# Weight loads and their waits moved into the norms' SyncE programs, and the last feed-forward layer storing its own output

## The reference, cut to what matters

```python
x = x + _L0_attn_a_ref(_layernorm(x, axis=-1), ...)
x = x + _L0_ffn_ref(_layernorm(x, axis=-1), ...)
x = x + _L0_attn_b_ref(_layernorm(x, axis=-1), ...)
x = x + _L0_ffn_ref(_layernorm(x, axis=-1), ...)
...
x = x + _L3_attn_b_ref(_layernorm(x, axis=-1), ...)
x = x + _L3_ffn_ref(_layernorm(x, axis=-1), ...)
return x
```

## Time and profile before

| | |
|---|---|
| Median of three runs | 3286.94 us |
| Lowest and highest | 3273.81 us, 3288.47 us |
| Profiled execution, its own time | 3289.86 us |
| Span of that execution, first to last instruction | 3288.1 us |
| Time outside the span | 1.76 us |
| Granted TensorE clock, mean over the span | 0.922 |
| TensorE busy, share of the span | 86% |
| VectorE, ScalarE, GpSimd busy | 56%, 42%, 23% |

### The profile page before, as it was taken

The page is one execution under the profiler, slowest core; times in us unless marked ns, Lnnn a source line. Parts: engine busy times, 40 slices in busy tenths (PEclk is TensorE's granted clock), DMA queues, the critical chain, the costliest instruction groups (busy, mean ns, idle before and its releaser), DMA issues. The chain is left out here.

```text
span 3288.1 us, 54460 instructions
## 1 busy us (share of the span) xinstructions
PE 2822.4 (86%) x21112; PEld 1419.8 (43%) x21112; DVE 1848.9 (56%) x3584; ACT 1366.0 (42%) x2665; POOL 765.5 (23%) x725
## 2 busy tenths in 40 slices
PE   6667788999988888899678888998889898889988
PEld 3454465333466433344322222342233444565546
DVE  4425553798763688311598888212594544537633
ACT  3314244422243376632367677422204232234552
POOL 1000063365354200000653230002550001230003
PEclk9779599899999899999789999998899998898989
DMA  3031011122012311000312100000430001031102
GB/s 119 16 100 47 13 42 48 60 70 67 11 49 87 76 30 27 2 0 0 66 26 34 24 12 1 1 0 15 112 103 0 1 1 52 21 101 36 33 2 78
DMA packets 84392, 130.03 MB, mean 40 GB/s; under 512 B 15584, under 2 KB 52928, under 8 KB 82856
## 3 DMA queue, kind: packets, MB, share of 16 engines
q1 hardware_dynamic: 71528, 106.68, 12.1%
q0 software_dynamic: 9152, 16.71, 2.1%
q10 hardware_dynamic: 3456, 3.15, 0.3%
HBM read 99.93 MB, written 25.85 MB: 38 GB/s over the span
## 5 line engine op out<-in xcount | busy, mean ns | idle before, releaser
L1811 DVE TENSOR_REDUCE at_mp<-PS 128x1 f32<-128x384 f32 (+3 forms) x640 | 307.0, 535 | 94.6 <-PE PS L1632 82.7
L1760 ACT ACTIVATE at_pt<-PS 128x384 f32<-128x384 f32 (+3 forms) x704 | 272.5, 455 | 198.0 <-PE PS L1632 163.7
L1624 PE MATMUL PS<-at_kx,at_qx 48*128 48x384 bf16 (+5 forms) x640 | 203.1, 354 | 37.2 <-DVE at_mp L1811 21.6
L113 PE MATMUL PS<-zeros 128*128 128x512 bf16 x834 | 208.6, 396 | 1.2 <-DVE mx_y L982 1.2
L1652 PE MATMUL PS<-at_qx,at_kx 57*128 57x512 bf16 (+5 forms) x704 | 196.5, 320 | 9.8 <-ACT at_pt L1760 9.4
L4335 ACT ACTIVATE ls_pt<-PS,ls_far 128x512 f32<-128x512 f32 x256 | 155.4, 684 | 22.5 <-PE PS L4156 18.1
L1632 PE MATMUL PS<-at_above,identb 64*128 64x128 bf16 (+1 forms) x1408 | 164.4, 216 | 0.0
L4482 DVE CUSTOM_DVE_ANT_0 PS<-PS,ls_pt 128x1024 f32<-128x1024 f32 x128 | 153.7, 1239 | 18.1 <-ACT ls_pt L4335 15.5
L1632 PE MATMUL PS<-at_other,at_eye 64*128 64x128 bf16 (+1 forms) x1408 | 162.2, 213 | 0.0
L2540 DVE TENSOR_TENSOR_SCAN mb_ring<-PS,mb_ring 128x1024 f32<-128x1024 f32 x64 | 146.6, 2290 | 18.9 <-POOL mb_ring L2473 6.7
L1133 DVE SCALAR_TENSOR_TENSOR X<-PS,small_L,X 128x512 f32<-128x512 f32 x8 | 6.0, 750 | 261.2 <-PE PS L1080 261.2
(11 more groups left out here) (839 smaller groups left out, 6330.6 us busy)
## 6 DMA issues: line engine op xcount, KB each, us to landing
rw_arena<-rw_v_rows SPq DMA_DIRECT2D x32, 512.0 KB, 4.7
dl_arena<-in_fir_bank SPq DMA_DIRECT2D x32, 256.0 KB, 3.2
lnA<-mb_rows SPq DMA_DIRECT2D x16, 512.0 KB, 3.7
XN<-mb_rows SPq DMA_DIRECT2D x16, 512.0 KB, 3.7
ffn_place<-in_ffn_L SPq DMA_DIRECT2D x4, 1152.0 KB, 17.0
x_rows<-mx_t SPq DMA_DIRECT2D x16, 256.0 KB, 2.5
mx_s<-y_rows SPq DMA_DIRECT2D x16, 256.0 KB, 5.0
ffn_place<-in_ffn_L SPq DMA_DIRECT2D x4, 1024.0 KB, 8.0
```

Of the source, the lines that this page charges most:

```text
L113: k.nc.tensor.matmul(k.PS[:, bank, :], k.zeros16[:, 0:P], k.zeros16[:, :], start=start, stop=start, skip_group_check=True)
L1624: mm = nc.tensor.matmul(PS[:, n % 3, 0:e - c], QX[rows, u % 3, g, blk(i, P)], KX[rows, u % 3, g, c:e], start=True, stop=True)
L1760: nc.scalar.activation(PT[:, y % SLOTS, g, 0:e - c], PS[:, 3 + n % 3, 0:e - c], ACT.Exp, scale=SCALE).then_inc(exp_done, 1)
L1811: nc.vector.tensor_reduce(best, sc, AX.X, ALU.max).then_inc(s_maxed, 1)
```

## The change

It does three things.

- `weights_beside` is a new SyncE program inside `layernorm` and `layernorm_twice`. If a group's weights are due to be loaded (`k.ffn_next`), it issues the four DMAs there, in the norm of the next sub-layer. Otherwise, if the sub-layer is a feed-forward layer (`k.ffn_due`), it waits there for the loads. Otherwise it does nothing.
- The three stages of `load_ffn` after feed-forward layers and the eight stages of `await_loads` ahead of feed-forward layers go. The load at the start and the two waits at the start stay.
- When the last sub-layer is `l3_ffn`, its SyncE program stores each block of `X` as soon as VectorE has added it, with two more semaphores in that stage (`x_done`, `stored`); the stage "stored" at the end goes. In `l3_ffn`, VectorE's wait behind each of the four adds becomes one wait behind all four.

```diff
+def weights_beside(k, sp):
+
+    if k.ffn_next is not None:
+        layer, k.ffn_next = k.ffn_next, None
+        n = pack_columns(FFN_W[layer])
+        for c in range(LOAD_PARTS):
+            part = slice(c * n // LOAD_PARTS, (c + 1) * n // LOAD_PARTS)
+            sp.dma_start(k.ffn_place[:, part], k.ins["ffn_" + layer][:, part]).then_inc(k.ffn_loaded, 16)
+        k.ffn_count += 16 * LOAD_PARTS
+    elif k.ffn_due:
+        sp.wait_ge(k.ffn_loaded, k.ffn_count)
...
+        @block.sync
+        def _(sp):
+            weights_beside(k, sp)
...
+                if k.last_output is not None:
+                    for b in range(NBLK):
+                        sp.wait_ge(x_done, b + 1)
+                        sp.dma_start(k.last_output[:, blk(b)], k.X[:, blk(b)]).then_inc(stored, 16)
+                    sp.wait_ge(stored, 16 * NBLK)
...
-                    own(nc.vector.tensor_tensor(k.X[:, blk(b)], k.X[:, blk(b)], PS[:, b, :], ALU.add))
+                    nc.vector.tensor_tensor(k.X[:, blk(b)], k.X[:, blk(b)], PS[:, b, :], ALU.add).then_inc(x_done, 1)
+                dve.wait_ge(x_done, NBLK)
...
-            if name.endswith("ffn"):
-                await_loads(k, k.ffn_loaded, k.ffn_count)
+            k.ffn_due = name.endswith("ffn")
+            k.last_output = out if i == last - 1 and name == "l3_ffn" else None
             with ExitStack() as layer:
                 run[name](k)
             if name.endswith("ffn") and i + 2 < last and SUBLAYERS[i + 2] != name:
-                load_ffn(k, SUBLAYERS[i + 2][0:2].upper())
-        with stage(nc, "stored") as (block, stored):
-            @block.sync
-            def _(sp):
-                for b in range(NBLK):
-                    sp.dma_start(out[:, blk(b)], k.X[:, blk(b)]).then_inc(stored, 16)
-                sp.wait_ge(stored, 16 * NBLK)
+                k.ffn_next = SUBLAYERS[i + 2][0:2].upper()
+                weight_views(k, k.ffn_place, FFN_W[k.ffn_next])
+        if k.last_output is None:
+            with stage(nc, "stored") as (block, stored):
...
```

More of the change, by code:

```diff
@@ L318, in l3_ffn @@
                    "rows_stored", "x_turned", "x_copied", "hid_ready", "hid_done", "y_ready", "y_taken",
-                   "diag_made", "block_0", "block_1", "block_2", "block_3", "mixed", "own_d") as (
+                   "diag_made", "block_0", "block_1", "block_2", "block_3", "mixed", "x_done", "stored", "own_d") as (
                        block, cleared, logits_ready, shifted, exp_done, picked, ranked, counted, in_tile, in_place, named, numbered, found, placed, turned, rows_copied,
                        rows_stored, x_turned, x_copied, hid_ready, hid_done, y_ready, y_taken,
-                       diag_made, block_0, block_1, block_2, block_3, mixed, own_d):
+                       diag_made, block_0, block_1, block_2, block_3, mixed, x_done, stored, own_d):
             back = (block_0, block_1, block_2, block_3)
@@ L4656, in program @@
     k = Core(nc)
-    k.ins, k.ffn_count = ins, 0
+    k.ins, k.ffn_count, k.ffn_next = ins, 0, None
     k.filled_count, k.fetched_count = 0, [0] * 8
@@ L4699, in program, with _ @@
             if name.endswith("ffn") and i + 2 < last and SUBLAYERS[i + 2] != name:
-                load_ffn(k, SUBLAYERS[i + 2][0:2].upper())
-        with stage(nc, "stored") as (block, stored):
-            @block.sync
-            def _(sp):
-                for b in range(NBLK):
-                    sp.dma_start(out[:, blk(b)], k.X[:, blk(b)]).then_inc(stored, 16)
-                sp.wait_ge(stored, 16 * NBLK)
+                k.ffn_next = SUBLAYERS[i + 2][0:2].upper()
+                weight_views(k, k.ffn_place, FFN_W[k.ffn_next])
+        if k.last_output is None:
+            with stage(nc, "stored") as (block, stored):
+                @block.sync
+                def _(sp):
+                    for b in range(NBLK):
+                        sp.dma_start(out[:, blk(b)], k.X[:, blk(b)]).then_inc(stored, 16)
+                    sp.wait_ge(stored, 16 * NBLK)
 def layout(inputs):
```

## The result

The changed kernel took 3262.44 us (median of 8 runs, 3253.16 to 3265.36) where the kernel before took 3287.66 us (8 runs, 3273.81 to 3293.07). The ratio is 0.9932, 95% interval 0.9912 to 0.9952: 22 us less. The forecast was 16.0 us less and 3271 us; 3262 us lies in the stated range of 3259 to 3281. Two repeats of the changed kernel gave 0.9934 (0.9912 to 0.9956) and 0.9922 (0.9900 to 0.9944).

What follows compares the result with a forecast made beforehand. TensorE is busy 86% of the span, but boundaries, where every engine idles, were what the change touches. Stages and stores 12.1 us plus clock 3.9 us gave 16.0 us less than 3286.94: 3271 us, range 3259 to 3281.

Steps and rivals of the forecast that it cites:

- The stages' length: At eleven boundaries, removing the eight awaiting stages saves 2.8 us and the three loading stages 7.0 us.
- the one that was priced apart: The awaiting stage into the second l2_ffn, said to cost 0.65 us where the other seven cost 0.31 each.
- The end: At the program's end, storing each block once added saves 2.3 us, between 1.7 and 2.5.
- The 0.2 us for stores beside the row loads: In the last l3_ffn, a row load behind a store could land late; 0.2 us taken off the end's 2.5.
- the forecast's signs of being wrong: A norm longer than its twin through SyncE, line 432 waiting over 0.54 us for `mx_yg`, or as many norms at 0.8 clock.
- The clock at the loads: Norms behind the loading boundaries regain clock: 2.5 us at l3a, 0.1 at l2a, 0 at l1a.
- The clock at the waits: Norms behind the eight awaiting boundaries regain clock with 0.31 us less idle time: 1.3 us, between −1 and 5.4.
- a quarter of the 5.4, 1.3 us: First l3_ffn's and first l2_ffn's norms, near an edge, could each win 2.7 us; a quarter of both was taken.
- rival C: The clock gives more, both edge norms and l1a's stay at 1.00: 21.6 us less, 3265 us; chance 0.18.
- Rival B: The clock gives nothing, falls are dealt out anew: 12.1 us less, 3275 us, up to 3281; chance with E 0.28.
- D: Not faster: clock falls land in stretches bound by TensorE, deciding from 12.1 us of such stretches; chance 0.04.
- E: The weight load runs into l1a's main stage and holds its DMAs: 1 to 3 us off the 12.1; chance with B 0.28.

Runs made afterwards that it cites:

- e1_loads: The kernel before with only the three weight loads moved into the norms, awaiting stages and storing stage kept: ratio 0.9967, 10.8 us less.
- e2_waits: The kernel before with only the eight waits moved into the norms, loading stages and storing stage kept: ratio 0.9971, 9.5 us less.
- e9_before_fill: The kernel before, all small stages kept, plus products of zeros on TensorE behind the last matmuls of eight kinds of sub-layer: ratio 0.9976, 7.9 us less.
- e4_warm_loads: The kernel before with nine products of zeros on TensorE inside each of the three loading stages, no stage removed: ratio 0.9985, 4.9 us less.
- c2_after: The changed kernel repeated unaltered under another name: 3259.8 us, ratio 0.9934 against the kernel before.
- e6_fill: The changed kernel plus products of zeros on TensorE behind sub-layers' last matmuls, beside VectorE's last adds: 3252.32 us, ratio 0.9912 against the kernel before.
- c1_before: The kernel before repeated unaltered under another name: 3281.41 us, ratio 0.9996.
- e3_end: The kernel before with only the last layer's own stores changed, all small stages of the loads kept: ratio 1.0001.
- e5_empty: The changed kernel with empty stages (a barrier and nothing in it) put back at the eleven boundaries: ratio 0.9962 against the kernel before.
- e10_empty_front: The changed kernel with eleven empty stages in a row ahead of the first sub-layer: ratio 0.9949 against the kernel before.

## Why the prediction was right, and which term was too small

**The stages' length** held. The boundaries of the changed kernel show 0.33 us less at an awaiting stage (0.85 to 0.52 into the first l3_ffn) and 0.66 at the one that was priced apart (1.19 to 0.53). 2.8 us for the waits and 7.0 for the loads were read off the boundaries, the boundaries came out as forecast (1.27 us into l3a, 2.90 into l1a), and e1_loads alone gave 10.8 us where the sum had 7.0 + 2.5 + 0.1 = 9.6 for that part. The moved DMAs were hidden in the norm as argued, at 357 GB/s, and nobody waited for SyncE.

**The end** was sized at 2.3 us and measured 5.36 − 2.8 = 2.5 us. The 0.2 us for stores beside the row loads can't be seen in the traces. One of the forecast's signs of being wrong did come up: line 459 waited 0.72 us for `mx_yg` in the changed kernel. It says nothing, because without the new stores the same matmuls waited 0.99 us in e2_waits and 0.62 in e9_before_fill.

**The clock at the loads** was sized at 2.6 us. The loads' stretches went from 44.3 to 34.5 us, 9.8 us, of which 7.0 are the stages: 2.8 us of clock. l3a's 2.5 us came in every trace of the changed kernel, l2a's norm stayed at GpSimd's 11.7, and l1a's gave little, as said. e4_warm_loads shows the cause at l3a, on one trace; e9_before_fill's norm there, with a shorter idle time and the stage in place, is at 10.3 us too.

**The clock at the waits** is the term that was mis-sized. The prediction took "a quarter of the 5.4, 1.3 us". The waits' stretches went from 106.6 to 99.1 us, 7.5 us, of which 2.8 are the stages: 4.7 us of clock, with the standard error of 1.8. The step looked for norms near an edge by the idle time ahead of them and found two. It passed over the first l1_ffn's and the second l3_ffn's, both with 0.79 us of idle time, behind an attention layer whose tail already ran at the low level. Over the same traces they went from 12.1 to 10.3 and from 12.7 to 10.8 us with their stages, so beyond the 0.31 us some 1.5 us each. And of the two it named, it took a quarter for both alike, where the first l3_ffn's norm went from 12.1 to 10.3 us and was at 1.00 in every trace without the stage, while the first l2_ffn's went from 11.9 to 11.5 only.

That the idle time at these very boundaries did it is shown less well than the sum. The 8 us ahead of the first l1_ffn's and the second l3_ffn's norm, in the kernel before and in the changed one (two and two windows, columns as in the earlier trace rows):

```profile
1378.40:1386.40 8.00, 5.46 (x12) 1.70 (x10) 1.38 (x2) 0.60 (x1) 0.00 (x0) 0.50 0.00 0
3184.20:3192.20 8.00, 5.44 (x11) 1.66 (x9) 1.50 (x2) 0.60 (x1) 0.00 (x0) 0.50 0.00 0
...
1370.50:1378.50 8.00, 4.10 (x16) 1.76 (x16) 1.75 (x4) 1.24 (x3) 0.00 (x0) 1.00 0.00 0
3163.40:3171.40 8.00, 5.72 (x12) 1.72 (x10) 1.50 (x2) 0.66 (x2) 0.06 (x1) 0.50 0.00 0
```

Into the second l3_ffn the tail is low in both, and the clock rises sooner in the norm of the changed kernel (0.93 over it, not 0.80). Into the first l1_ffn the clock fell over 7 us ahead of the norm, so the boundary behind can't have started the fall: it fell there in all seven traces with the stage and in only two of the seven without (c2_after, e6_fill). At most the boundary can delay the return; why the tail kept the clock in the other five is not shown. The first l3_ffn's norm was low in only three of the seven traces with its stage (before, c1_before, e3_end), and in those l3a's norm was low too. In e1_loads, e4_warm_loads, e5_empty and e9_before_fill it ran at 1.00 with the stage in place. Part of its gain may thus belong to the loads' side of the change.

With 7.5 + 9.8 + 2.5 the three parts add up to 19.8 us, where the ratio of 0.9932 is 22.4 us of 3287.66 (interval 15.8 to 28.9). The sum is between the forecast's 16.0 and rival C's 21.6 us, with other norms than C named; the interval of the time holds both. Rival B, the clock gives nothing, would leave 12.1 us, which lies outside that interval, and the stretches of both parts speak against it. D and E did not happen. The Trainium skill says in TensorE: Matmul & The Clock Gate (section What's actually happening) that the number of matmuls at the low clock differs between runs of one kernel. The traces agree, since c1_before's norms fell out otherwise than those of before, but the mean moved all the same.

**What stays open.** l3b's main stage, which the change does not touch, took 225.7 to 227.9 us in all six traces without a stage ahead of the feed-forward layers and 230.1 to 243.3 in the seven with one; e10_empty_front, made to tell why, gave 229.4. The difference is in how long the clock stays low in it: the granted clock over it was 0.87 in the kernel before, 0.92 in the changed one and 0.83 in e1_loads, the longest. The means are 235.6 and 227.1 us, 8.5 us in favour of the change, of which the sum above leaves room for 2.6, or for 9.1 at the upper end of the interval. The other main stages did not grow to make up for it: but for the last one, they sum to 0.7 us less in the six traces, with a standard error of 2.6. A clean split of thirteen traces into these seven and six would come by chance once in 1716 ways. The grouping was made after the traces were seen, so the odds are less extreme than that, but chance is the weaker reading. What in the change would do it was not found, and e1_loads and e2_waits may hold part of it in their times. This open piece is larger than any of the clock terms.

## What to carry to other kernels

Price a barrier at a boundary twice: its own length (0.31 to 0.33 us here), and what TensorE's clock does around it. Here the second was 4.7 us, give or take 1.8, against 2.8 for the eight waits. On one trace and a time that leans its way (e9_before_fill), part of it can be had back without removing anything, by products of zeros beside the tail of another engine. For small effects of the clock sum the touched stretches over several traces; a single trace picked the wrong norms.

## What the runs showed of the hardware that was not expected

- Over the runs of one kernel the span goes with the clock: 33 runs of the kernel before, a slope of 0.59 us of span for each us of span × (1 − clock). Three other sets of it, 16 to 23 runs each, gave 0.58 to 0.61; the other kernels, 6 to 12 runs each, 0.41 to 0.83. With a standard deviation of 10.8 us in that lost time, the slope of the 33 runs makes 6.4 of the 7.5 us by which the span spreads.
- The clock can be low at a boundary with little idle time: the first l1_ffn's norm, stage included, took 10.9 to 13.1 us in the seven traces with a stage there, though TensorE idled only 0.79 us ahead of it, and 10.33 or 10.34 us in the seven without. With the stage the clock had fallen over 7 us ahead of the norm, in a tail in which TensorE worked with gaps (5.46 of 8 us busy in the kernel before).
- 256 KB stores, the first of them issued beside row loads of the same size, landed 2.2 to 4.5 us after their issue in seven traces, where four in a row behind the last add took 2.2 to 3.0, and they did not hold up the loads by an amount that thirteen traces can show.
